# A chain of four modulated convolutions: the first product in three parts, composed blocks evened out, stores put off

## What is computed

```python
def _layer(x, style, w, b, mw, mb, typ):
    s = style @ mw.T + mb
    weight = SCALE * w * s[:, None, :, None]
    demod = lax.rsqrt(jnp.sum(weight * weight, axis=(2, 3)) + EPS)
    weight = weight * demod[:, :, None, None]
    if typ == 'same':
        out = jax.vmap(_conv_same)(x, weight) + b[None, :, None]
    elif typ == 'upsample':
        out = jax.vmap(_conv_up)(x, weight.transpose(0, 2, 1, 3)) + b[None, :, None]
        out = _blur(out, 2.0 * blur_k, (1, 1))
    elif typ == 'downsample':
        xb = _blur(x, blur_k, (2, 2))
        out = jax.vmap(_conv_down)(xb, weight) + b[None, :, None]
# types of the four layers: 'same', 'upsample', 'same', 'downsample'
# x = x + layer3(layer2(layer1(layer0(x))))
```

## Time and profile before

| | |
|---|---|
| median of three runs | 181.44 us (180.81 to 181.85) |
| the profiled execution | 181.34 us, its span 179.2 us |
| TensorE busy | 170.8 us, 95% |
| VectorE busy | 125.4 us, 70% |
| ScalarE busy | 57.2 us, 32% |
| GpSimd busy | 15.4 us, 9% |
| mean granted TensorE clock | 0.980 |

### The profile page before, as it was taken

How to read it: one execution, slowest core, us unless ns; L and a number is a source line. 1 busy time by engine, 2 the same in 40 slices (tenths; PEclk the granted TensorE clock), 3 DMA queues, 4 the chain that set the end, 5 groups by cost and what they waited for, 6 DMA issues and landing times.

```text
span 179.2 us, 7986 instructions
## 1 busy us (share of the span) xinstructions
PE 170.8 (95%) x3567; PEld 155.4 (87%) x3567; DVE 125.4 (70%) x265; ACT 57.2 (32%) x126; POOL 15.4 (9%) x47
## 2 busy tenths in 40 slices
PE   7899999999999799999999999999999999999990
PEld 5598969986677498999999999999999999998960
DVE  7659755896776946758494949494949394958793
ACT  3433554122142233324151514243332424222110
POOL 7002202800001300200000000000000000000000
PEclk9958999999999999999999999999999999999999
DMA  4960003033000986827274645456463637333322
GB/s 135 365 75 2 4 0 91 4 89 123 0 5 4 273 278 240 225 88 222 98 170 161 159 166 152 177 115 214 103 224 91 237 89 236 93 121 75 140 117 117
DMA packets 11778, 23.65 MB, mean 132 GB/s; under 512 B 5184, under 2 KB 5728, under 8 KB 11744
## 3 DMA queue, kind: packets, MB, share of 16 engines
q1 hardware_dynamic: 11680, 23.12, 42.8%
q10 hardware_dynamic: 64, 0.02, 0.1%
HBM read 8.85 MB, written 8.39 MB: 96 GB/s over the span
## 4 chain that ended last, share of the span: by engine, by line
PE 91%; DVE 3%; issue 2%; ACT 1%; DVEq 0%
PE p_m L415 26%; PE p_le L354 14%; PE p_lo L354 13%; PE p_le L398 12%; PE p_m L433 11%; PE p_lo L385 5%; PE p_le L304 2%; PE p_m L294 1%; PE p_le L402 1%; PE p_m L512 1%; PE p_m L505 1%; DVE r_sb L769 1%; PE p_m L285 1%; PE p_m L343 1%; PE p_m L495 1%
## 5 line engine op out<-in xcount | busy, mean ns | idle before, releaser
L415 PE MATMUL p_m<-u,Hw 64*64 64x256 f32 x896 | 61.0, 377 | 0.3 <-DVE z_sb L787 0.3
L415 PEld LDWEIGHTS p_m<-u,Hw 64*64 64x64 f32 x896 | 46.9, 132 | 2.6 <-issue 0.5
L354 PE MATMUL p_lo<-xin,w0s 64*64 64x259 f32 x384 | 31.0, 406 | 0.0
L736 DVE SCALAR_TENSOR_TENSOR Hw<-p_le,pvec,Hw 128x320 f32<-128x320 f32 x16 | 8.8, 551 | 31.0 <-ACT Hw L605 31.0
L354 PE MATMUL p_le<-xin,w0s 64*64 64x260 f32 x384 | 30.1, 407 | 0.2 <-DVE Hw L743 0.2
L398 PE MATMUL p_le<-R_sb,F_st 64*64 64x192 f32 x320 | 30.0, 324 | 0.0
L398 PEld LDWEIGHTS p_le<-R_sb,F_st 64*64 64x64 f32 x320 | 25.8, 133 | 1.1 <-issue 0.4
L354 PEld LDWEIGHTS p_lo<-xin,w0s 64*64 64x64 f32 x384 | 21.8, 137 | 2.4 <-issue 0.3
L354 PEld LDWEIGHTS p_le<-xin,w0s 64*64 64x64 f32 x384 | 20.7, 137 | 3.4 <-issue 1.1
L605 ACT ACTIVATE Hw<-p_le,pvec 128x448 f32<-128x448 f32 x16 | 10.2, 635 | 37.0 <-PE p_le L398 37.0
L787 DVE SCALAR_TENSOR_TENSOR z_sb<-p_m,pvec,s_sb 128x512 f32<-128x512 f32 (+1 forms) x30 | 21.0, 742 | 0.9 <-PE p_m L415 0.9
(11 more groups left out here) (122 smaller groups left out, 155.9 us busy)
## 6 DMA issues: line engine op xcount, KB each, us to landing
xin<-in_x_dram SPq DMA_DIRECT2D x16, 512.0 KB, 4.8
out_dram<-ot SPq DMA_DIRECT2D x16, 512.0 KB, 5.4
Hw<-Hw SPq DMA_DIRECT2D x30, 192.0 KB, 3.0
wn<-in_L_cond_weights_dram SPq DMA_DIRECT2D x1, 192.0 KB, 3.5
mwn<-in_L_cond_mod_w_dram SPq DMA_DIRECT2D x1, 128.0 KB, 2.3
xe<-in_x_dram SPq DMA_DIRECT2D x2, 56.0 KB, 8.2
cn<-in_cond_dram ACTq DMA_DIRECT2D x1, 16.0 KB, 2.1
bn<-in_L_cond_mod_b_dram ACTq DMA_DIRECT2D x1, 1.0 KB
```

The lines of the kernel that those rows point to most:

```text
L354: ins = pe.matmul(bank[h * C:(h + 1) * C, s, 0:n], w0s[p % 2][rows, k, :], xin[p % NX][rows, i0:i0 + 2 * n - 1:2], start=(k == 0), stop=(k ...
L415: ins = pe.matmul(bank(h)[s * C:(s + 1) * C], tap(p, h, s, blk), u[p % 2][h * C:(h + 1) * C, s, j, k:k + NM], start=(k == 0), stop=(k == l ...
```

## The change

- The first product no longer takes four blocks of 256 columns. It is three parts of 128 columns: two on differences in a larger `uu`, stage `product_1`, and one on every second column of `u`, stage `product_1_mid`, into a free piece of `p_lo`. `make_uu` makes twice as much, in two instructions, and stands ahead of `add_parts`. `add_mid` adds the middle part to `s`; the next turn's `layer0_odd` waits for it.
- `compose_H` takes the last column block for the first three taps on the lower rows instead of the upper ones; a GpSimd copy (`F_dup`) supplies the weights there.
- `compose_R(p + 2)` goes ahead of `product_2(p)`, and `compose_H(p + 2)` ahead of the edges. ScalarE's loop is not in the diff.
- The last demodulation (`W_D3`) is no longer applied to each product but in `add_x`, to the whole; `W_C` is divided by it. The last pair is finished like the others, its even half ahead of `product_3`.
- The sums of the blocks go from VectorE to GpSimd (but for pair 0) and are one more; TensorE waits for `H_added` instead of them. GpSimd's preparation for the edges changes its order.
- SP holds the stores of the first pairs back: none in turns 0 to 2, two a turn in turns 3 to 5.

```diff
     NM, NQ = 256, 128
-    BASE = 506
+    BASE = 508
...
+F_st = sb("F_st", [P, NF + 3, C])
 V_st = sb("V_st", [P, K, C])
 G_mv = sb("G_mv", [P, K, C])
...
+def sum_blocks(eng, p):
+    eng.wait_ge(H_added, p + 1)
+    w = Hw[p % NW]
+    eng.tensor_tensor(w[:, 0, 9:6:-1], w[:, 0, 2:7:2], w[:, 0, 1:6:2], ALU.add).then_inc(H_sums1, 1)
+    eng.tensor_tensor(w[:, 0, 12:14], w[:, 0, 6:1:-4], w[:, 0, 4::-4], ALU.add).then_inc(H_sums, 1)
+    eng.wait_ge(H_sums1, p + 1)
+    eng.tensor_tensor(w[:, 0, 10], w[:, 0, 7], w[:, 0, 8], ALU.add).then_inc(H_sums, 1)
+    eng.tensor_tensor(w[:, 0, 11], w[:, 0, 9], w[:, 0, 0], ALU.add).then_inc(H_sums, 1)
...
-    pool.wait_ge(made["s0"], 1)
-    pool.wait_ge(e_loaded, 32)
...
+    pool.wait_ge(made["e2"], 1)
+    pool.wait_ge(w_loaded, 16)
     pool.wait_ge(zeroed, 7)
...
-    pool.wait_ge(made["oep"], 2)
-    for p in range(PAIRS):
+    pool.wait_ge(copied["F_st"], 1)
+    pool.tensor_copy(F_st[C:P, NF:], F_st[0:C, 0:3]).then_inc(made["F_dup"], 1)
...
+    def put_edges(p):
+        pool.wait_ge(made["oep"], 2)
         wait(pool, stored[p % NO_T], 16 * (p // NO_T))
...
+    sum_blocks(pool, 1)
+    for p in range(PAIRS):
+        if p + 2 < PAIRS:
+            sum_blocks(pool, p + 2)
+        for q in range(LATE) if p == LATE - 1 else (p,) if p >= LATE else ():
+            put_edges(q)
...
-        sp.wait_ge(H_sums, 2 * (p + 1))
+        sp.wait_ge(H_sums, 3 * (p + 1))
...
     def store(p):
-        if p < PAIRS - 1:
-            sp.wait_ge(out_made, p + 1)
-        else:
-            sp.wait_ge(z_made, 2 * PAIRS)
+        sp.wait_ge(out_made, p + 1)
         sp.wait_ge(edge_put, p + 1)
...
-        store(p)
+        if LATE - 1 <= p < 2 * LATE - 2:
+            store(2 * (p - LATE + 1))
+            sp.wait_ge(H_done, p + 4)
+            store(2 * (p - LATE + 1) + 1)
+        if p >= 2 * LATE - 2:
+            store(p)
...
             pe.wait_ge(R_evac, 2 * (p + 1))
+        wait(pe, e_made, p - 1)
         layer0(p, p_lo, NO, 1, lo_done)
...
-        wait(pe, H_sums, 2 * min(p + 1, PAIRS))
+        wait(pe, H_added, min(p + 1, PAIRS))
         layer0(p, p_le, NE, 0, le_done)
...
-        for b, (even, odd) in enumerate(((((0, 2), 0), ((1,), 0)),
-                                         (((1,), 1), ((0, 2), 0)),
-                                         (((0, 2), 1), ((1, 3), 1)))):
+        for b, (even, odd) in enumerate((((slice(0, 3, 2), 0, 2), (slice(1, 2), 0, 1)),
+                                         ((slice(1, 2), 1, 1), (slice(0, 3, 2), 0, 2)),
+                                         ((slice(0, 3, 2), 1, 2), (slice(1, 3), 1, 2)))):
...
-        wait(pe, H_sums, 2 * p)
+        wait(pe, H_added, p)
...
         for c in range(NF):
             for s in range(2):
-                ins = pe.matmul(p_H[s * C:(s + 1) * C, c * C:(c + NR) * C], F_st[0:C, c, :],
-                                R_sb[s][0:C, 0:NR].rearrange("p a c -> p (a c)"), start=(c == 0),
-                                stop=(c == NF - 1), skip_group_check=True)
+                part(p_H, 0, s, c, 0, 2 if c < 3 else 3, c, start=(c == 0), stop=(c == NF - 1))
                 if c < NF - 1:
-                    pe.matmul(p_Ho[s * C:(s + 1) * C, (c + 1) * C:(c + NR) * C], F_st[C:P, c, :],
-                              R_sb[s][C:P, 0:NR - 1].rearrange("p a c -> p (a c)"), start=(c == 0),
-                              stop=(c == NF - 2), skip_group_check=True)
+                    part(p_Ho, 1, s, c, 0, 2, c + 1, start=(c == 0), stop=False)
+        if p == 0:
+            pe.wait_ge(made["F_dup"], 1)
+        for c in range(3):
+            for s in range(2):
+                ins = part(p_Ho, 1, s, NF + c, 2, 1, c + 2, start=False, stop=(c == 2))
         ins.then_inc(H_done, 1)
...
-        wait(pe, s_made, 2 * p)
...
+        wait(pe, s_made, p)
+        w, ww = u[p % 2], uu[p % 2]
+        part(p, lambda h: p_m2[:, h, 0:NQ], (10, 11),
+             lambda rows, s, k: w[rows, s, 1, 2 * k + 1:2 * k + 2 * NQ:2])
+        pe.wait_ge(uu_made, 2 * (p + 1))
+        part(p, lambda h: p_m2[:, h, NQ:2 * NQ], (7, 9), lambda rows, s, k: ww[rows, s, 1, 0, k:k + NQ])
+        part(p, lambda h: p_m2[:, h, 2 * NQ:3 * NQ], (8, 0), lambda rows, s, k: ww[rows, s, 1, 1, k:k + NQ])\
+            .then_inc(m2_done, 1)
     def product_1(p):
+        if p < PAIRS - 1:
+            wait(pe, z_made, 2 * p)
+        bank = p_m13[:, :, 0] if p < PAIRS - 1 else p_le
+        ww = uu[p % 2]
+        part(p, lambda h: bank[:, h, 0:NQ], (6, 2), lambda rows, s, k: ww[rows, s, 0, 0, k:k + NQ])
+        part(p, lambda h: bank[:, h, NQ:2 * NQ], (4, 0), lambda rows, s, k: ww[rows, s, 0, 1, k:k + NQ])\
+            .then_inc(m1_done, 1)
+    def product_1_mid(p):
         pe.wait_ge(ud_made, p + 1)
+        pe.wait_ge(uo_made, min(p + 2, PAIRS))
+        pe.wait_ge(R_evac, 2 * min(p + 3, PAIRS))
+        wait(pe, e_made, p)
+        w = u[p % 2]
+        part(p, lambda h: p_lo[:, h, 2 * NQ:3 * NQ], (12, 13),
+             lambda rows, s, k: w[rows, s, 0, 2 * k + 1:2 * k + 2 * NQ:2]).then_inc(mid_done, 1)
+    def product_3(p):
         wait(pe, z_made, 2 * p)
-        product(p, lambda h: p_m13[:, h, 0, 0:NM], 0, (6, 4, 2, 0))
-    def product_3(p):
         product(p, lambda h: p_m13[:, h, 1, 0:NM], 2, (5, 3, 1)).then_inc(m13_done, 1)
...
-        product_2(p)
         if p + 2 < PAIRS:
             compose_R(p + 2)
+        product_2(p)
         if p == 0:
             pe.wait_ge(made["c"], 2)
         product_1(p)
+        if p + 2 < PAIRS:
+            compose_H(p + 2)
         if p < 3:
-            pe.wait_ge(s_made, 2 * (p + 1))
+            pe.wait_ge(s_made, p + 1)
         if p == 0:
             edge_x0()
         if p == 1:
             edge_y()
         if p == 2:
             edge_out()
-        if p + 2 < PAIRS:
-            compose_H(p + 2)
+        product_1_mid(p)
         product_3(p)
         if p == 1:
             edge_z()
...
-        wait(act, s_made, 2 * (p - 1))
-        act.activation(t_sb[p % 2][:], p_m2[:, :, 0:NQ], ACT.Identity, scale=pcol(W_D3, p), bias=pcol(W_C, p))\
+        wait(act, s_made, p - 1)
+        act.activation(t_sb[p % 2][:], p_m2[:, :, 0:NQ], ACT.Identity, bias=pcol(W_C, p))\
            .then_inc(t_made, 1)
...
-        dve.wait_ge(H_added, p + 1)
...
     def make_uu(p):
         dve.wait_ge(uo_made, p + 1)
...
+        dve.wait_ge(ud_made, p + 1)
+        wait(dve, m13_done, p - 1)
+        for s in range(2):
+            even = u[p % 2][:, s, 0:2, 0:NO:2]
+            even = bass.AP(even.tensor, even.offset, [list(even.ap[0]), list(even.ap[1]), [2, 2], [2, NQ + 1]])
+            dve.tensor_tensor(uu[p % 2][:, s], even,
+                              u[p % 2][:, s, 0:2, 1:NO:2].unsqueeze(2).to_broadcast([P, 2, 2, NQ + 1]),
+                              ALU.subtract).then_inc(uu_made, 1)
     def add_parts(p):
         dve.wait_ge(t_made, p + 1)
         wait(dve, z_made, 2 * (p - 1))
...
+        dve.tensor_tensor(s_sb[p % 2][:].rearrange("p h (b j) -> p h b j", b=2),
+                          p_m2[:, :, NQ:3 * NQ].rearrange("p h (b j) -> p h b j", b=2),
+                          t_sb[p % 2][:].unsqueeze(2).to_broadcast([P, 2, 2, NQ]), ALU.add).then_inc(s_made, 1)
+    def add_mid(p):
+        dve.wait_ge(mid_done, p + 1)
+        dve.wait_ge(s_made, p + 1)
+        wait(dve, z_made, 2 * p)
+        dve.tensor_tensor(e_sb[:].rearrange("p h (b j) -> p h b j", b=2),
+                          p_lo[:, :, 2 * NQ:3 * NQ].unsqueeze(2).to_broadcast([P, 2, 2, NQ]),
+                          s_sb[p % 2][:].rearrange("p h (b j) -> p h b j", b=2), ALU.add).then_inc(e_made, 1)
     def finish(p):
+        def parity(a, part, add):
+            to = z_sb[p % 2][:, :, a::2].rearrange("p h (j b) -> p h b j", b=2)
+            dve.tensor_tensor(to, part, add[:].rearrange("p h (b j) -> p h b j", b=2), ALU.add)\
+               .then_inc(z_made, 1)
         last = p == PAIRS - 1
-        to = ot[p % NO_T] if last else z_sb[p % 2]
-        dve.wait_ge(m13_done, p + 1)
-        dve.wait_ge(s_made, 2 * (p + 1))
         if last:
-            dve.wait_ge(r_made, 2)
-            wait(dve, stored[p % NO_T], 16 * (p // NO_T))
+            dve.wait_ge(m1_done, p + 1)
         else:
-            wait(dve, out_made, p - 1)
-        for h in range(2):
-            n0, m0 = EDGE + h * BASE, 3 * h
-            add = r_sb[:, h, :, m0:] if last else s_sb[p % 2][:, h, m0:].unsqueeze(1).to_broadcast([P, 2, NM - m0])
-            dve.scalar_tensor_tensor(out=to[:, n0 + 2 * m0:n0 + 2 * NM].rearrange("p (m a) -> p a m", a=2),
-                                     in0=p_m13[:, h, :, m0:NM], scalar=pcol(W_D3, p), in1=add,
-                                     op0=ALU.mult, op1=ALU.add).then_inc(z_made, 1)
+            dve.wait_ge(m13_done, p + 1)
+        dve.wait_ge(e_made, p + 1)
+        wait(dve, out_made, p - 1)
+        even = p_le[:, :, 0:NM] if last else p_m13[:, :, 0]
```

(26 more changed lines are left out.)

101 lines of the change are left out of this document (39 added, 62 removed).

## The result

The kernel after takes 192.05 us (median of four runs, 191.98 to 192.31) against 181.2 for the one before on the same chip (180.81 to 181.85): the ratio is 1.060, 95% interval 1.056 to 1.063, 10.9 us slower. The forecast was 185.5, with a range up to 190.0. The profiled execution has a span of 190.3 against 179.2, 11.1 more.

What follows compares the result with a forecast made beforehand. TensorE was taken to bound the kernel, 91% of the chain. Steady turns +2.9, turns that differ +0.9, start +0.4 and end 0 make +4.2 us on 181.34, so 185.5 us, range 180.5 to 190.0.

Steps and rivals of the forecast that it cites:

- the sum of a steady turn: One turn of the pair loop: -0.34 - 0.20 + 0.70 + 0.05 = +0.21 us, +2.9 over 14 turns.
- the start: Before the loop: shorter waits against VectorE's added work and GpSimd beside it, +0.4 us, between -1.0 and +1.0.
- the end: Turn 14 gains 0.34 us; VectorE's last piece grows from 6.38 to 6.73, +0.35; together 0.
- The pause ahead of H: Between product_2 and H: TensorE stands still 0.70 us a turn (0.5 to 0.9), as evac_R stays behind scale_2.
- Rivals 1 and 2: 1: no pause ahead of H, 175.7 us, chance 0.10; 2: pause about 0.5, start wins 1.0, 181.2 us, chance 0.12.
- The stages: In a steady turn: first product gains 0.34 us in three parts, H evened out 0.20, R's new place costs 0.05.
- The two parities 1.37: In VectorE's last piece after the last product of pair 14: the two parity instructions take 1.37 us together.
- Turns 0, 2 and 3: Odd waits 1.35 us (turn 0), 1.2 (turn 2) for add_mid; ze comes later, +0.4; turn 3's product_2 wait goes, -1.56.
- Rival 3: VectorE late in every turn: add_mid delays e, 0.25 us reaches odd each turn, 3.5 more, 189.0 us; chance 0.12.

Runs made afterwards that it cites:

- e1_act: The kernel after with ScalarE's R copies (evac_R) put ahead of scale_2: 184.25 us, ratio to the kernel before 1.017.
- e4b_evenH: The kernel before with H evened out and nothing else of the change: 178.22 us, 0.982.
- e5_pool: e1_act with GpSimd's order at the start put back and the edge products only after turn 0's edge: 183.47 us, 1.011.
- e3_nostore: The kernel after without the output transfers of pairs 3 to 14: 189.27 us, 1.046.
- e8_actnostore: e1_act without the output transfers of pairs 3 to 14: 183.25 us, 1.010.
- e11_fill32: e1_act with 32 needless matmuls in the start, moving later instruction-transfer borders by half a transfer: 194.80 us.
- e12_fill16: e1_act with 16 needless matmuls in the start, moving later instruction-transfer borders by a quarter of a transfer: 186.84 us, 1.030.
- e13_act64: e1_act with 64 fillers in the start spread over four tiles, one whole instruction transfer: 183.88 us, 1.014.
- e9_evenR: The kernel before with H evened out, R ahead of the second product and the R copies ahead of scale_2: 178.28 us, 0.984.
- e2_split: The kernel before with each 256-column matmul of the first product issued as two of 128, order unchanged: 184.06 us, 1.016.
- e10_hold: e4b_evenH with the stores of the first pairs held back, leaving two a turn from turn 3: 175.61 us, 0.970.
- e6_natural: e1_act with s and e stored in natural order, so finish writes every second float: 185.98 us, 1.024.

## Why the prediction was wrong

The direction and the pause that was to decide were right; the size was not, 10.9 against 4.2 us, and the time lies 2 us beyond the range. The step that failed is the sum of a steady turn, which had TensorE's work and its waits on semaphores and put the supply of its instructions at nothing: 4.1 us. The terms of the start (2.0 too small) and of the end (1.8) were mis-sized as well. Against them the stages got shorter than forecast by some 1.6 us in turns 4 to 13, an error that hid a part of the others.

- **The pause ahead of H: right, and shown.** Forecast 0.70, measured 0.73 to 0.76 in 13 turns and 0.88 in turn 0, and e1_act takes it away by ScalarE's order alone. Rivals 1 and 2 fall.
- **The stages: right in kind, too small.** H 1.33 against 1.37 forecast and 1.60 before. e4b_evenH puts its gain at 0.33 a turn instead of 0.20. By the clean turn of e1_act, 8.5 against e4b_evenH's 8.99, the other parts bring another 0.5, where the prediction had 0.34 for m1 and nothing for R. Together about 0.8 against 0.54. Not all of it shows in the kernel after: its clean turn of 9.37, less the pause of 0.74, is 8.63. A turn of 9.37 is also 0.05 over the kernel before and not the 0.21 of the sum.
- **What the sum didn't have: the supply of instructions.** The prediction said of a steady turn that TensorE's own work and its semaphore waits are all there is, "Net of a steady turn: ... +0.21". For turns 4 to 13 that gave +2.1; +5.2 were measured: 4.1 of pauses for instructions, 0.5 of ten times 0.05, and 0.6 in turns 8 and 12. No rival named them. More and shorter matmuls stood in the diff, and the page of before had the queue's row (28 packets, 32 after); I passed over it, for there it cost nothing.
- **The start: +0.4 forecast, -1 to +1, and +2.4 measured.** The term was priced as VectorE's added work and GpSimd's neighbours. What it was: GpSimd's order costs 1.8, small VectorE instructions that wait out its longer ones, 0.66 instead of 0.18 (e1_act against e5_pool), and 0.8 is the clock at half from 23.1 to 26.5, which the prediction didn't have. The rest, -0.2 together, is VectorE's added work against what the shorter H and the dropped sums save, and a demodulation that starts 0.3 later. The prediction had GpSimd's mechanism beside rival 3, by the page's rule, with a price of +1.0 at most: it was named, and its price was too small. The same start with the full clock at that place (e3_nostore, e8_actnostore) has +1.0 and +1.2.
- **The end: 0 forecast, +1.8 measured.** "The two parities 1.37" took the time of half a finish for an instruction that writes with another step. They take 1.11 and 1.11 for pair 14, and 1.06 and 1.05 for pair 15, as here in the timeline of VectorE in the kernel after:

```profile
179.07 1.11 DVE L828 TENSOR_TENSOR z_sb<-p_m,e_sb 128x512 f32<-128x512 f32 x1
180.02 1.11 DVE L828 TENSOR_TENSOR z_sb<-p_m,s_sb 128x512 f32<-128x512 f32 x1
...
183.92 1.06 DVE L828 TENSOR_TENSOR z_sb<-p_le,e_sb 128x512 f32<-128x512 f32 x1
184.82 1.05 DVE L828 TENSOR_TENSOR z_sb<-p_m,s_sb 128x512 f32<-128x512 f32 x1
185.91 1.28 DVE L851 SCALAR_TENSOR_TENSOR ot<-z_sb,pvec,xin 128x1018 f32<-128x1018 f32 x1
```

  VectorE's last piece runs from 179.07 to 187.19, 8.1 us against 6.73 forecast; the four parities are 1.3 of the 1.4.
- **Turns 0, 2 and 3: close.** Odd waited 1.35 and 1.37, forecast 1.35 and 1.2; turn 3's wait of 1.56 is gone. R in turn 2 waited 1.21 for ze, where m2 waited 0.35 before: 0.86 more and not 0.4. These are the rows of weight loads of the kernel after:

```profile
38.66 0.47 PEld L381 LDWEIGHTS p_lo<-xin,w0s 64*64 64x64 f32 x12 [1.35 <-issue]
...
55.04 0.54 PEld L413 LDWEIGHTS p_lo<-A_sb,V_st 64*64 64x64 f32 x24 [1.21 <-DVE ze L746]
...
63.62 1.16 PEld L381 LDWEIGHTS p_lo<-xin,w0s 64*64 64x64 f32 x24 [1.37 <-issue]
```

- **Rival 3 (VectorE late in every turn)** didn't come: outside turns 0 and 2 no row has odd waiting for `e`.

What is shown and what is not: that the pauses stand at the borders between packets of instructions rests on 81 of them in the traces of 16 kernels. That their borders' place moves them rests on e11_fill32, e12_fill16 and e13_act64. That most of them come with the first product in parts rests on e9_evenR against e1_act, which differ in that, in the sums on GpSimd, in the last demodulation and in the order of the start and the stores. Which property of this product does it stays open. Pairs per microsecond go with the pauses roughly: up to 25.0 they come to 1.7 us at most, at 26.1 to 2, at 27.9 and 28.2 to 6.5 to 11.2; the kernel after and e3_nostore, at 27.8 outside the wait ahead of H, have 4.1 and 1.0. How fast the densest stretch goes isn't enough: 128 pairs on end take 3.5 us at the least in e2_split, 3.4 in e1_act, 4.2 in e10_hold and 4.6 before. What differs is how early the packets start, 202 records ahead in the median in e2_split and 148 in e1_act. What makes a packet start late stays open; the output transfers aren't it in e1_act's case, for without them (e8_actnostore) it is 146.

## What to carry to other kernels

Where TensorE is busy all the time with matmuls of 128 columns and less, count its instructions as a load of its own: look at the instruction queue's row, and at waits with no releaser in the middle of a product. Take a change apart and time its parts: here H evened out and held stores gain 5.5 us, and the other parts, with ScalarE's order left as it was, cost 16.4. An instruction that another engine's queue order makes late (the R copies behind scale_2) has to move with the work that it serves.

## What the runs showed of the hardware that was not expected

- A 16 KB packet holds 256 of TensorE's instructions (all 81 pauses stand at the same place of a block of 256). It takes 0.9 to 2.6 us by its record, and starts at most 293 records ahead of its border. TensorE goes on 1.2 to 1.9 us after its end, 0.9 to 1.2 in seven cases, in six of which the packet took over 2 us. Pauses of 0.15 us or more run up to 2.2.
- After a wait of 2.26 us TensorE's granted clock was 0.50 (the 1.2 GHz level) for 3.4 us in the kernel after, and 48 loads of H took 2.44 us instead of 1.31. After a wait of 1.56 in e3_nostore it stayed at 1.00.
- Around e1_act's pauses in H (from 98 to 119 us) the packets start 3.9 to 4.2 and 5.9 to 6.2 us apart by turns; in e2_split over the same stretch 4.3 to 4.9.
- VectorE writing 512 fp32 values takes 1.08 us with a step of 16 bytes and 0.69 with one of 8 (the kernel after against e6_natural).
- 64 pairs of 64-column matmuls take 88 ns each on one tile (e11_fill32); in the stages that use four tiles short ones start every 21 to 28 ns.
